# The last member of each group of four is picked by VectorE's own sums instead of by a TensorE product

## What is computed

```
def _sparsify_2to4(h):
    g = h.reshape(B, S, I // 4, 4)
    a = jnp.abs(g)
    _, idx = jax.lax.top_k(a, 2)
    mask = (pos == idx[..., 0:1]) | (pos == idx[..., 1:2])
    return (g * mask).reshape(B, S, I)
h = jax.nn.silu(x @ w_gate) * (x @ w_up)          # I = 2048
x = x + 0.5 * (_sparsify_2to4(h) @ w_down)
```

```
h = exp(d_l * A) * h + (d_l * u_l) * b_l ;  y_l = sum_n h * c_l
```

## Time and profile before

| | |
|---|---|
| median of three runs | 3607.98 us (3605.13 to 3610.43) |
| the profiled execution | 3602.44 us, span 3600.7 us |
| TensorE busy | 3360.2 us, 93% |
| VectorE busy | 3027.7 us, 84% |
| GpSimd busy | 2594.9 us, 72% |
| ScalarE busy | 2061.7 us, 57% |
| granted TensorE clock, mean | 0.979 |

### The profile page before, as it was taken

One profiled execution on the slowest core, in us unless ns is written; L12 is line 12 of the kernel. 1 busy time (PEld: TensorE's weight loads), 2 busy tenths in 40 slices (PEclk: granted clock), 3 DMA queues, 4 the chain that ended last, 5 costly groups with the idle time before them and its releaser, 6 DMA issues. The chain is left out here.

```text
span 3600.7 us, 39012 instructions
## 1 busy us (share of the span) xinstructions
PE 3360.2 (93%) x11958; PEld 2122.7 (59%) x12020; DVE 3027.7 (84%) x3597; ACT 2061.7 (57%) x2805; POOL 2594.9 (72%) x1625
## 2 busy tenths in 40 slices
PE   8999999999999999999999999988989889988899
PEld 6775566556655665566555565555545555555467
DVE  5546998788999889988898899988998988999934
ACT  5546657567565765566565675565555566454422
POOL 1316876667877779768787678868888878979913
PEclk9999999999999999999999999999999989999999
DMA  9656566657756676566665675647646556645433
GB/s 356 219 188 192 176 207 222 205 176 221 215 175 210 202 227 200 171 203 208 187 205 176 202 230 169 221 138 215 222 124 210 172 178 220 187 149 184 139 120 114
DMA packets 243470, 696.45 MB, mean 193 GB/s; under 512 B 23536, under 2 KB 23792, under 8 KB 233584
## 3 DMA queue, kind: packets, MB, share of 16 engines
q1 hardware_dynamic: 173632, 559.72, 45.1%
q10 hardware_dynamic: 69632, 134.23, 15.6%
HBM read 619.94 MB, written 76.55 MB: 193 GB/s over the span
## 5 line engine op out<-in xcount | busy, mean ns | idle before, releaser
L1381 POOL TENSOR_TENSOR scan_in<-du,scan_rows 128x512 f32<-128x512 f32 x1024 | 1312.8, 1294 | 700.9 <-DVE decay L1255 612.1
L1255 DVE TENSOR_TENSOR_SCAN decay<-decay,scan_in 128x512 f32<-128x512 f32 x1024 | 1252.4, 1223 | 157.0 <-ACT decay L865 150.9
L865 ACT ACTIVATE decay<-delta,small 128x512 f32<-128x512 f32 x1024 | 699.4, 689 | 935.4 <-DVE scan_out L1265 928.7
L1394 POOL TENSOR_TENSOR y<-y,scan_out 128x1024 f32<-128x1024 f32 x512 | 1227.0, 2397 | 0.6 <-DVE scan_out L1265 0.6
L637 PE MATMUL main<-zhi,wunit 128*128 128x512 f32 x2048 | 909.9, 444 | 62.1 <-DVE cmp L1195 38.3
L729 PE MATMUL side<-h,wdown 128*128 128x512 f32 x1760 | 801.8, 599 | 24.2 <-ACT sq L988 12.6
L639 PE MATMUL main<-zhi,wunit 128*128 128x512 f32 x2048 | 817.7, 399 | 0.0
L638 PE MATMUL main<-zlo,wunit 128*128 128x512 f32 x2048 | 816.7, 399 | 0.0
L1265 DVE TENSOR_TENSOR scan_out<-decay,scan_rows 128x512 f32<-128x512 f32 x1024 | 702.9, 686 | 27.6 <-POOL y L1394 2.2
L729 PEld LDWEIGHTS side<-h,wdown 128*128 128x128 f32 x1760 | 334.5, 191 | 392.7 <-issue 350.2
L637 PEld LDWEIGHTS main<-zhi,wunit 128*128 128x128 f32 x2048 | 390.2, 191 | 233.6 <-issue 89.5
(11 more groups left out here) (117 smaller groups left out, 3192.8 us busy)
## 6 DMA issues: line engine op xcount, KB each, us to landing
wunit<-hl_dram SPq DMA_DIRECT2D x480, 512.0 KB, 4.3
scan_rows<-bc_dram ACTq DMA_DIRECT2D x256, 512.0 KB, 5.7
wdown<-down_w_dram SPq DMA_DIRECT2D x256, 256.0 KB, 3.2
wmam<-mam_dram SPq DMA_DIRECT2D x128, 512.0 KB, 4.1
hl_dram<-wunit SPq DMA_DIRECT2D x32, 512.0 KB, 4.6
skip_dram<-skb SPq DMA_DIRECT2D x64, 256.0 KB, 4.2
delta<-skip_dram SPq DMA_DIRECT2D x16, 1024.0 KB, 6.7
wmam<-wout_dram SPq DMA_DIRECT2D x32, 512.0 KB, 4.3
```

The lines of the kernel that those rows point to most:

```text
L865: nc.scalar.activation(decay[u % BANKS][:], delta[:, e, :], ACT.Exp, scale=aneg[:, e * N + n:e * N + n + 1]).then_inc(sem["decay_ready"], 1)
L1255: nc.vector.tensor_tensor_scan(decay[u % BANKS][:], decay[u % BANKS][:], db[u % INPUTS][:], 0.0, ALU.mult, ALU.add).then_inc(sem["state_re ...
L1381: nc.gpsimd.tensor_tensor(db[u % INPUTS][:], du[:, e, :], rows[m % ROWS][:, 0, :], ALU.mult).then_inc(sem["input_ready"], 1)
L1394: nc.gpsimd.tensor_tensor(y[:, e:e + 2, :], y[:, e:e + 2, :], scan_out[:, k:k + 2, :], ALU.add).then_inc(sem["sum_ready"], 1)
```

## The change

For the 61 steps that are not in `COUNTED`, the side job of member 3 is gone, with its three matmuls. VectorE adds plane 4 to plane 3 of `cmp`, in place, ahead of the selection of member 2, adds plane 5 to it behind that selection, and then selects member 3 from that plane (`select_last`), which is in SBUF, where before the sum came from a PSUM bank. The down products, the next step's first comparison into `cmp`, and ScalarE's copy of member 3 in the edge steps wait for the new semaphore `last_selected`. With 61 side jobs fewer, the others take other banks in turn, and `place_units`, whose code is unchanged, counts three `win` where it counted four.

```diff
@@ -75,6 +75,12 @@
 
 COUNTED = EDGE[AHEAD_OF_SCANS:-1]
 
+
+def place_of(s):
+    return s - sum(c < s for c in COUNTED)
+
+
+
 LEAD = 8
 
 STARTS = (67, 130, 190, 250, 310, 363, 409, 454, 516)
@@ -125,7 +131,7 @@
 
 
         for s, base in enumerate(self.base):
-            for j in range(4 if s not in COUNTED else 0):
+            for j in range(3 if s not in COUNTED else 0):
                 self.jobs_at[base + WIN_TICKS[j]].append(("win", s, j))
             for t in range(KD):
                 self.jobs_at[base + DOWN_TICKS[t]].append(("down", s, t))
@@ -343,7 +349,7 @@
 
         sem = {name: ctx.enter_context(nc.semaphore(name)) for name in (
             "product_ready", "side_ready", "gate_read", "up_read", "part_ready",
-            "magnitude_ready", "compared", "counted", "selected",
+            "magnitude_ready", "compared", "counted", "selected", "added", "last_selected",
             "member_high_ready", "member_split_ready", "down_high_ready", "down_split_ready",
             "centred_tile", "squared_tile", "scaled_tile", "squares_ready", "quarter_ready", "root_ready", "scaled", "high_part_ready", "normed_ready",
             "decay_ready", "input_ready", "state_ready", "weighted_ready", "sum_ready",
@@ -372,6 +378,8 @@
 
             if s in COUNTED:
                 eng.wait_ge(sem["selected"], 4 * COUNTED.index(s) + j + 1)
+            elif j == 3:
+                eng.wait_ge(sem["last_selected"], place_of(s) + 1)
             else:
                 wait_read(eng, ("win", s, j))
 
@@ -696,7 +704,7 @@
                 if j == 0:
                     pe.wait_ge(sem["compared"], 3 * s + 3)
                 for k, (c, sign) in enumerate((((0, 0), (1, 0), (3, 0)), ((0, 1), (2, 0), (4, 0)),
-                                               ((1, 0), (2, 0), (5, 1)), ((3, 0), (4, 0), (5, 0)))[j]):
+                                               ((1, 0), (2, 0), (5, 1)))[j]):
                     mm = nc.tensor.matmul(bank[:], signs[:, sign, :], cmp[:, c, :], start=(k == 0), stop=(k == 2))
                 mm.then_inc(sem["side_ready"], 1)
 
@@ -722,8 +730,9 @@
                 _, s, t = key
                 bank = side_bank(key)
                 if t == 0:
-                    for j in range(4):
+                    for j in range(3):
                         wait_read(pe, ("win", s, j))
+                    pe.wait_ge(sem["last_selected"], place_of(s) + 1)
                 pe.wait_ge(sem[f"down_loaded_{t}"], 16 * (s + 1))
                 for j in range(4):
                     mm = nc.tensor.matmul(bank[:], wdown[t][:, j, :], h[s % 2][:, j, :], start=(j == 0), stop=(j == 3))
@@ -1189,7 +1198,7 @@
                 first = j * (j - 1) // 2
                 dve.wait_ge(sem["magnitude_ready"], pair + 1)
                 if j == 1 and s and s - 1 not in COUNTED:
-                    wait_job(dve, ("win", s - 1, 3))
+                    dve.wait_ge(sem["last_selected"], place_of(s - 1) + 1)
                 if j == 1 and s - 1 in COUNTED:
                     dve.wait_ge(sem["selected"], 4 * COUNTED.index(s - 1) + 4)
                 nc.vector.tensor_tensor(cmp[:, first:first + j, :], ab[:, 0:j, :], main[(gate_of(pair) + 2) % MAINS][:].unsqueeze(1).broadcast_to([P, j, L]),
@@ -1198,10 +1207,24 @@
             def select(key):
 
                 _, s, j = key
-                op, least = ((ALU.is_ge, 2.0), (ALU.is_ge, 1.0), (ALU.is_le, 0.0), (ALU.is_le, 1.0))[j]
+                op, least = ((ALU.is_ge, 2.0), (ALU.is_ge, 1.0), (ALU.is_le, 0.0))[j]
                 wait_job(dve, key)
                 nc.vector.scalar_tensor_tensor(h[s % 2][:, j, :], bank_of(key)[:], least, h[s % 2][:, j, :], op,
                                                ALU.mult).then_inc(read_of(key), 1)
+
+            def add_last(s, k):
+
+                n = place_of(s)
+                wait_job(dve, ("win", s, 2))
+                if k:
+                    dve.wait_ge(sem["added"], 2 * n + 1)
+                nc.vector.tensor_tensor(cmp[:, 3, :], cmp[:, 3, :], cmp[:, 4 + k, :], ALU.add).then_inc(sem["added"], 1)
+
+            def select_last(s):
+                n = place_of(s)
+                dve.wait_ge(sem["added"], 2 * n + 2)
+                nc.vector.scalar_tensor_tensor(h[s % 2][:, 3, :], cmp[:, 3, :], 1.0, h[s % 2][:, 3, :], ALU.is_le,
+                                               ALU.mult).then_inc(sem["last_selected"], 1)
 
             def count_and_select(s):
 
@@ -1318,7 +1341,11 @@
                 begin(share(units, 0, 4))
                 for key in jobs:
                     if key[0] == "win":
+                        if key[2] == 2:
+                            add_last(key[1], 0)
                         select(key)
+                        if key[2] == 2:
+                            add_last(key[1], 1)
                     if key[0] == "down":
                         add_down(key)
                     if key[0] == "out":
@@ -1327,6 +1354,9 @@
                         centre(key)
                 if compared is not None and compared < PRODUCTS // 2 - 1:
                     compare(compared)
+                for key in jobs:
+                    if key[0] == "win" and key[2] == 2:
+                        select_last(key[1])
                 finish(share(units, 0, 4))
                 for i, j in edge_members(tick):
                     if i == len(EDGE) - 1:
```

## The result

The changed kernel takes 3704.28 us (median of 4 runs, 3702.89 to 3710.19) against 3606.56 us before, beside it on the same chip: a ratio of 1.0279, 95% interval 1.0266 to 1.0292, or 98 us slower. The forecast was 54 us slower, 3662 us, with a range to 3720 us.

What follows compares the result with a forecast made beforehand. TensorE was taken to bound early, both engines in the middle, VectorE late. Late +42, middle +12, between +3, first steps -3 gave +54 us: 3656 us on the profiled execution, 3662 us as median, range 3606 to 3720 us.

Steps and rivals of the forecast that it cites:

- the late stage: From 2000 to 3420 us: VectorE leads; 24 steps x 2.6 us = 62 us added, +42 us after cover.
- TensorE's gain: Three matmuls fewer, 0.66 us a step, 40 us over 61 steps at most; late it was put at nothing.
- the middle: From 430 to 2000 us: 28 steps x 2.0 us = 56 us added, 44 us covered by waits for TensorE, +12 us.
- VectorE's own additions: The two additions a step cost VectorE 0.67 us, without GpSimd's waits.
- The waits for GpSimd: Instructions with two SBUF operands wait for GpSimd: first addition 0.5 us middle, 1.1 late; second run 0.8 us in both.
- the last selection go free: Last selection, in one run with the second addition, waits for GpSimd no further and stays near 0.69 us.
- 1.1 to 1.4 as the sign: Sign to look for: the 122 additions have a mean of 1.1 to 1.4 us with scans, not 0.42.
- the third rival: GpSimd also comes in between last addition and last selection: +68 us, 3730 us; chance 0.13.
- 12 + 8 us be covered late: From 2000 us on, VectorE's waits cover 12 us (for TensorE) and 8 us (for the decay) of 62 added.
- the first four: First four changed steps: TensorE leads and no down product waits for a selection, 4 x -0.66 = -3 us.
- The moved scan units: Scan units that change their tick: priced at 0, between a gain and a loss of some us.
- the last selection's wait for its own sum: Last selection needs the addition right ahead: 0.08 us a step, 5 us in all at most, taken as 0.

Runs made afterwards that it cites:

- e10: Changed kernel without the two additions, member 3 picked by member 2's sum from its PSUM bank, three matmuls still gone: 3592.15 us, ratio 0.9961 to the kernel before.
- e9: Changed kernel with no new instruction having two SBUF operands, additions halved to 256 columns, and TensorE's three matmuls kept: 3638.85 us, ratio 1.0094 to the kernel before.
- e3: Changed kernel, but TensorE still does member 3's three matmuls, into member 2's bank: 3718.45 us, ratio 1.0310 to the kernel before.
- e1: Changed kernel, but new instructions take one operand from member 2's PSUM bank and additions cover 256 columns: 3624.13 us, ratio 1.0046 to the kernel before.
- e4: Changed kernel, but the last selection reads plane 5 alone and needs no wait for the addition: 3707.57 us, ratio 1.0278 to the kernel before.
- e6: Changed kernel with member 2's selection first and both additions and the last selection in one row behind it: 3724.24 us, ratio 1.0328 to the kernel before.
- e2: Changed kernel with scan units dealt out as before, the planner still counting the fourth sum: 3706.32 us, ratio 1.0274 to the kernel before.
- e7: Changed kernel with four additions, 2.14 us a step on VectorE, and no new instruction with two SBUF operands: 3703.93 us, ratio 1.0271 to the kernel before.

## Why the forecast was right in kind and too small

**What bounds.** Right for the late stage, where VectorE's added time is paid in full and more, though TensorE's gain shows there too (6 us in e10, forecast 0). For the middle I had 44 of 56 us covered, as if TensorE led most of the time, and it did not: e9 and e3 show cover for 11 to 14 us, and the removal of all 183 matmuls brought 11 to 17 us of 40.

**VectorE's own additions, 0.67 us a step.** Not contradicted: e1's 0.41 us recorded, with 0.08 of overlap, is the same pace, though for 256 columns with one operand from PSUM; the shortest of the changed kernel's own, 0.40 us, agrees.

**The waits for GpSimd.** The mechanism was right, and e1 shows it. Their size was near too: from the means above, a step adds 2 x (785 - 80) + 1348 - 680 ns = 2.08 us in the middle (forecast 2.0) and 2 x (868 - 80) + 1425 - 680 = 2.32 us late (2.6). Where they lie was wrong: I let the last selection go free behind the second addition. It waits 0.67 us on average in the middle and 0.74 late, and the additions wait less than I had it, 0.37 and 0.45 us each: their mean is 0.79 to 0.87 us where I had named 1.1 to 1.4 as the sign. In the first steps they did not stay near 0.42 us either but had a mean of 0.88 (8 additions up to 195 us), since GpSimd has work of the edge steps there. That the price of a step came out within 0.3 us is luck in part: the wait put at nothing and the waits put too high made up for each other. So the third rival's mechanism is real (e4, e6), and its price was not on top of the others but in their place. The rows of four in the earlier trace rows ran on unhindered; I read this as a rule for rows. GpSimd had nothing ready there, as it waited for the next scan:

```profile
2698.42 1.29 POOL L1381 TENSOR_TENSOR scan_in<-du,scan_rows 128x512 f32<-128x512 f32 x1 [3.67 <-DVE decay L1255]
```

The port is given away between the instructions of a row (e4, e6). The Trainium skill ("SBUF — State Buffer", "SBUF: two separate sides") says that whoever starts first holds the shared pair for the whole instruction and the other is blocked, and the 2.72 us of the selection above agree.

**From VectorE's time to the kernel's: the term that was mis-sized.** This is the step of the forecast that failed: it let 12 + 8 us be covered late and 44 us in the middle, 64 us of 118. The steps' lengths, from the starts of the products' first weight loads: steps 8 to 35 got 36 us longer (forecast 12), steps 36 to 59 60 us (forecast 42), steps 4 to 7 4 us (3), the first four 2 us shorter (3). With 28 x 2.08 = 58 and 24 x 2.32 = 56 us added, the middle kept 22 us: 10 of them are what the removal alone brings there (e10), and the rest is cover, 11 to 14 us by e9 and e3, against the 44 of the forecast. Late nothing was covered, against 20. So the waits of VectorE for TensorE, and those for the decay late, were counted as cover that was not there. The waits in the middle say how (total us, times, longest), before:

```profile
PE main L637 <- DVE zlo L1159: 7.8, 4, 3.8
PE main L637 <- DVE cmp L1195: 5.6, 6, 1.9
```

and after:

```profile
DVE decay L1278 <- ACT decay L874: 75.1, 55, 4.9
PE main L645 <- DVE cmp L1204: 19.7, 10, 4.2
PE main L645 <- DVE zlo L1168: 16.3, 4, 6.5
DVE res_r L1263 <- PE side L738: 9.7, 7, 2.6
...
DVE res_r L1273 <- PE side L766: 6.8, 6, 2.5
DVE res_g L1263 <- PE side L738: 4.4, 7, 1.4
```

VectorE's waits for TensorE behind the down products fell from 27.7 to 9.7 us, so they did take something up; but TensorE's waits for VectorE's comparisons and low parts (`zlo`) grew from 13.4 to 36 us there. That a wait of VectorE for TensorE covers little because TensorE itself comes late from an earlier wait for VectorE fits with this, but I have not shown it by itself. Why the late steps lose more than what was added is not shown either; TensorE's lower clock there (last section) is one candidate.

**The moved scan units and the last selection's wait for its own sum** were priced at 0. The first is open within some us (e2). For the second, VectorE stood idle 1.9 us in all ahead of the 61 last selections, and without that wait (e4) the time was the same.

## What to carry to other kernels

Before work goes to VectorE beside a busy GpSimd, look at where its operands lie: two in SBUF make every such instruction wait for what GpSimd has under way, one from PSUM doesn't. Three short instructions of 1.3 us took 2.7 to 2.9 us so. Where two engines are each about 90% busy (here TensorE 97 and 89% of the two stages before, VectorE 88 and 92%) and wait for each other, don't count the waits of one for the other as cover: here 54 us of such waits in the middle covered 11 to 14, and late none, so that each us added per step cost 51 to 54 us over 56 such steps, at 0.67 us as at 2.1, while the 40 us taken off the other engine returned 11 to 17.

## What the runs showed of the hardware

- TensorE had 183 matmuls less and was busy 7 us longer. Its mean granted clock fell from 0.979 to 0.966, in the late stage from 0.96 to 0.94, while its waits grew (from 233 us in 130 waits to 325 us in 153). Of its two levels (1.2 and 2.4 GHz) the trace has the lower one for 150 us before and 249 us after. e3, with the same matmuls as before, shows the two apart:

```profile
PE 3411.3 (92%) x12020; PEld 2144.0 (58%) x12020; DVE 3156.7 (85%) x3719; ACT 2060.9 (55%) x2805; POOL 2607.1 (70%) x1625
```

There TensorE is busy 51 us longer than before, also with 249 us at the lower level, and the change is 44 us below it. So the removal brought its 40 us of busy time, and more waits with a lower clock took about as much back. With TensorE's part alone (e10) the clock was 0.974.

- Where GpSimd is the one that comes second, its instruction is recorded longer too: L1424 took 2.52 us in the step above, with a usual 2.4; it is held for the rest of a VectorE instruction, and e7 shows that this cost nothing here.
